# A two-layer graph network: the nodes normalised in eight groups of blocks instead of seven

## What is computed

```python
x = _layernorm(x + _L0_gnn_ref(edge_index, x))          # layer 0
x = _layernorm(x + _L1_gnn_ref(x, edge_index, edge_attr_4, edge_attr_32, ...))   # layer 1

# layer 0: out[dst] += x[src] * deg_inv_sqrt[src] * deg_inv_sqrt[dst]
# layer 1: w = relu(edge_feat @ W1 + b1) @ W2 + b2        four 8 x 8 matrices per edge
#          m = products of w, x[src] and edge_sh          32 numbers per edge
#          out[dst] += m ; out += x @ (si_w0, si_w1) / sqrt(8)

def _layernorm(x, eps=1e-05):
    m = jnp.mean(x, axis=-1, keepdims=True)
    v = jnp.var(x, axis=-1, keepdims=True)
    return (x - m) / jnp.sqrt(v + eps)
```

## Time and profile before

| | |
|---|---|
| runs | 3487.09, 3489.55, 3490.99 us (median 3489.55) |
| the profiled execution | 3488.94 us, its span 3486.2 us |
| TensorE busy | 2796.1 us, 80% of the span |
| VectorE busy | 2974.5 us, 85% |
| ScalarE busy | 1433.7 us, 41% |
| GpSimd busy | 2464.9 us, 71% |
| mean granted TensorE clock | 0.928 of full speed |
| table transfers after layer 0 | 7 of 224 KB |
| output transfers | 6 of 224 KB, one of 208 KB and one of 10.5 KB |

### The profile page before, as it was taken

How to read it: one execution, slowest core, us unless ns; L and a number is a source line. 1 busy time by engine, 2 the same in 40 slices (tenths; PEclk the granted TensorE clock), 3 DMA queues, 4 the chain that set the end, 5 groups by cost and what they waited for, 6 DMA issues and landing times.

```text
span 3486.2 us, 55367 instructions
## 1 busy us (share of the span) xinstructions
PE 2796.1 (80%) x17493; PEld 1893.0 (54%) x17493; DVE 2974.5 (85%) x6514; ACT 1433.7 (41%) x3154; POOL 2464.9 (71%) x2520
## 2 busy tenths in 40 slices
PE   5699999999999987777777787777778777877775
PEld 4477776777777764444444454444445444444443
DVE  8788888888888865988888889889889888988987
ACT  0788888888888863211121112111212121112211
POOL 0677776777777657777777777777777777777774
PEclk9999999999999997999898898999989998999988
DMA  2200000000000021111111111111111111111112
GB/s 50 29 14 14 13 14 13 14 14 13 12 14 14 13 34 22 31 27 28 27 31 27 27 27 31 27 27 28 30 27 28 27 31 27 27 28 27 31 27 34
DMA packets 181444, 85.57 MB, mean 25 GB/s; under 512 B 124024, under 2 KB 167608, under 8 KB 181176
## 3 DMA queue, kind: packets, MB, share of 16 engines
q0 software_dynamic: 79872, 41.05, 8.0%
q1 hardware_dynamic: 101304, 41.07, 5.2%
HBM read 77.13 MB, written 4.81 MB: 24 GB/s over the span
## 4 chain that ended last, share of the span: by engine, by line
POOL 39%; issue 17%; ACT 17%; PE 14%; DVE 12%; DVEq 1%; DMA 1%; POOLq 0%; SPq 0%; ACTq 0%
POOL xg L435 39%; ACT z_sb L476 9%; ACT q_sb L476 7%; PE ps L635 4%; PE ps L648 4%; PE ps L593 3%; DVE prod_all L1062 2%; DVE stage L1231 2%; PE ps L623 1%; DVE oh L949 1%; DVE prod_all L1221 1%; PE ps L739 1%; DVE sumT_all L1085 1%; DVE lane L1058 1%; DVE z_sb L841 1%
## 5 line engine op out<-in xcount | busy, mean ns | idle before, releaser
L435 POOL DMA_INDIRECT xg<-x_table,idx x1664 | 1602.5, 963 | 562.7 <-issue 531.4
L435 POOL DMA_INDIRECT xg<-scaled_x_table,idx x832 | 854.9, 1028 | 400.7 <-issue 374.5
L739 PE MATMUL ps<-w2t,hT 128*128 128x256 f32 x3328 | 899.8, 417 | 283.9 <-DVE prod_all L1221 278.9
L739 PEld LDWEIGHTS ps<-w2t,hT 128*128 128x128 f32 x3328 | 643.2, 204 | 735.7 <-issue 640.3
L635 PE MATMUL ps<-prod_all,lane 128*128 128x363 bf16 (+1 forms) x2496 | 792.5, 320 | 51.8 <-DVE prod_all L1062 35.0
L1062 DVE TENSOR_SCALAR prod_all<-wide_lane,key 128x363 bf16<-128x363 bf16 (+1 forms) x2496 | 730.4, 316 | 27.8 <-PE ps L635 23.0
L1231 DVE TENSOR_REDUCE stage<-prod_all 128x192 f32<-128x1536 f32 x416 | 724.0, 1741 | 0.2 <-issue 0.2
L523 ACT ACTIVATE hT<-ps,b 64x512 f32<-64x512 f32 x416 | 284.4, 684 | 932.7 <-PE ps L732 928.6
L476 ACT ACTIVATE q_sb<-ps 128x363 bf16<-128x363 f32 (+1 forms) x1248 | 504.7, 543 | 94.2 <-PE ps L635 87.8
L476 ACT ACTIVATE z_sb<-ps 128x363 bf16<-128x363 f32 (+1 forms) x1248 | 504.7, 543 | 85.1 <-PE ps L635 81.8
L1215 DVE TENSOR_TENSOR prod_all<-ps,stage 128x768 f32<-128x768 f32 x416 | 397.1, 955 | 143.6 <-PE ps L739 68.7
(11 more groups left out here) (128 smaller groups left out, 1528.5 us busy)
## 6 DMA issues: line engine op xcount, KB each, us to landing
efT<-in_efT SPq DMA_DIRECT2D x104, 256.0 KB
xg<-x_table,idx POOLq DMA_INDIRECT x1664
xg<-scaled_x_table,idx POOLq DMA_INDIRECT x832
sh<-in_sh SPq DMA_DIRECT2D x104, 32.0 KB
idx<-in_src SPq DMA_DIRECT2D x156, 8.0 KB
scaled_x_table<-q_sb SPq DMA_DIRECT2D x2, 784.0 KB, 7.6
x_table<-x_sb SPq DMA_DIRECT2D x7, 224.0 KB, 4.7
out_rows<-q_sb SPq DMA_DIRECT2D x6, 224.0 KB
```

Of the source, the lines that this page charges most:

```text
L435: pool.indirect_dma_start(rows[k][:, t, :], None, table, bass.IndirectOffsetOnAxis(ap=idx[k][:, t:t + 1], axis=0),).then_inc(s_g[layer][k] ...
L739: mm = pe.matmul(ps_w[j % 2][:, t, :], hT[j % 2][:, t * P:(t + 1) * P], w2t[:].rearrange("p c o i -> p (c o i)"), start=True, stop=True)
```

## The change

The group bounds are written out: `bounds = [0, 14, 28, 42, 56, 70, 84, 92, 98]`. Six groups of fourteen blocks stay; the seventh, once blocks 84 to 97, is now 84 to 91 (eight blocks), and an eighth holds the last six. All slices, the tests for the last output rows and the counts that depend on `NG` follow. `last_chunk_of(6)` is 98 and `turn_of(6)` is 50. Since the loop over the remaining groups in layer 0 now comes right behind a group that is scaled in the same buffer `z_row`, VectorE waits there for its own row.

```diff
+LAST = 6
...
-    NG = NP // GB
+    bounds = [*range(0, NP, GB), NP - LAST, NP]
+    NG = len(bounds) - 1
...
     def last_chunk_of(g):
-        return CHUNKS - 1 if g == NG - 1 else min(CHUNKS - 1, math.ceil((GB * P * (g + 1) + SLACK) / RISE) - 1)
+        return CHUNKS - 1 if g == NG - 1 else min(CHUNKS - 1, math.ceil((P * bounds[g + 1] + SLACK) / RISE) - 1)
...
         def blocks_of(t, g):
-            return t[:, g * GB:(g + 1) * GB, :]
+            return t[:, bounds[g]:bounds[g + 1], :]
...
-                for b in range(GB):
-                    col = (g * GB + b) * P
+                for b in range(bounds[g + 1] - bounds[g]):
+                    col = (bounds[g] + b) * P
                     mm = pe.matmul(ps_rows[:, b * D:(b + 1) * D], sumT[layer][:, col:col + P],
...
+            def first_rows(t, g):
+                return t[:, 0:bounds[g + 1] - bounds[g], :]
...
             def centre(layer, g, z):
-                cols = slice(g * GB, (g + 1) * GB)
+                cols = slice(bounds[g], bounds[g + 1])
                 dve.wait_ge(s_tr[layer], g + 1)
-                rows = ps_rows.rearrange("p (h f) -> p h f", f=D)
+                rows = first_rows(ps_rows.rearrange("p (h f) -> p h f", f=D), g)
...
                 for g in left:
-                    centre(0, g, z_row[:]).then_inc(s_last[0] if g == NG - 1 else s_var[0], 1)
-                    scale(0, g, z_row[:], g + 1)
+                    if g:
+                        dve.wait_ge(s_row[0], g)
+                    centre(0, g, first_rows(z_row, g)).then_inc(s_last[0] if g == NG - 1 else s_var[0], 1)
+                    scale(0, g, first_rows(z_row, g), g + 1)
```

More of the change, by code:

```diff
@@ L372, in _ @@
                 sp.wait_ge(s_row[1], g + 1)
-                a, b = g * GB, min((g + 1) * GB, full)
+                a, b = bounds[g], min(bounds[g + 1], full)
                 if b > a:
@@ L377, in _ @@
                     sent += 1
-                if a <= full < (g + 1) * GB and rest:
+                if a <= full < bounds[g + 1] and rest:
                     sp.dma_start(out_d[full * P:n_out, :], q_sb[0:rest, full, :]).then_inc(s_out, 16)
@@ L480, in deviations @@
             def deviations(layer, g):
-                cut = slice(g * GB, (g + 1) * GB)
+                cut = slice(bounds[g], bounds[g + 1])
                 act.wait_ge(s_var[layer], g + 1)
@@ L1002, in spread_over @@
             def spread_over(t, g):
-                return t[:, g * GB:(g + 1) * GB].unsqueeze(2).to_broadcast([P, GB, D])
+                return t[:, bounds[g]:bounds[g + 1]].unsqueeze(2).to_broadcast([P, bounds[g + 1] - bounds[g], D])
+            def first_rows(t, g):
+                return t[:, 0:bounds[g + 1] - bounds[g], :]
             def centre(layer, g, z):
-                cols = slice(g * GB, (g + 1) * GB)
+                cols = slice(bounds[g], bounds[g + 1])
                 dve.wait_ge(s_tr[layer], g + 1)
-                rows = ps_rows.rearrange("p (h f) -> p h f", f=D)
+                rows = first_rows(ps_rows.rearrange("p (h f) -> p h f", f=D), g)
                 if layer == 0:
@@ L1019, in centre @@
                     out=z, in0=spread_over(mean, g), scalar=-1.0 / D, in1=z, op0=ALU.mult, op1=ALU.add)))
-                dve.wait_ge(s_node[layer], link(layer, dve.tensor_tensor(z_sq[:], z, z, ALU.mult)))
-                return dve.tensor_reduce(var[:, cols], z_sq[:], AX_X, ALU.add)
+                dve.wait_ge(s_node[layer], link(layer, dve.tensor_tensor(first_rows(z_sq, g), z, z, ALU.mult)))
+                return dve.tensor_reduce(var[:, cols], first_rows(z_sq, g), AX_X, ALU.add)
             def scale(layer, g, z, made):
-                cols = slice(g * GB, (g + 1) * GB)
+                cols = slice(bounds[g], bounds[g + 1])
                 dve.wait_ge(s_std[layer], made)
@@ L1147, in _ @@
                     if centred:
-                        scale(0, centred[0], z_row[:], centred.pop() + 1)
+                        scale(0, centred[0], first_rows(z_row, centred[0]), centred.pop() + 1)
                     if left and turn_of(left[0]) == n - 1:
                         g = left.pop(0)
-                        centre(0, g, z_row[:]).then_inc(s_var[0], 1)
+                        centre(0, g, first_rows(z_row, g)).then_inc(s_var[0], 1)
                         centred.append(g)
```

## The result

The changed kernel takes 3477.86 us (median of seven runs, 3475.76 to 3480.64) beside 3489.55 us for the kernel before (3485.6 to 3492.56), a ratio of 0.9967 with a 95% interval of 0.9955 to 0.9979. The forecast was 3479.8 us. Measured twice more in later sittings it is 0.9974 (0.9964 to 0.9984) and 0.9976 (0.9967 to 0.9985), so the first ratio lies on the high side of the gain, and 8 to 9 us are the better figure. The profiled execution is the fastest of the seven: 3475.76 us, its span 3473.7 us.

A forecast was written before the change was run, and what follows sets the result against it. GpSimd's layer 1 gathers were taken as the bound: -4.6 us at layer 0's end, 0 inside layer 1, -5.0 at the program's end, -9.6 from 3488.94; with 0.6 us to the median, 3479.8 us, range 3477.0 to 3484.0.

The forecast's parts named there:

- The bound: GpSimd's uninterrupted gather stream in layer 1 leads; gains come from the end of layer 0 and the end of the program.
- Tiles' start: End of layer 0: the group of eight goes ahead of the last sixteen dense tiles, delaying their start, +2.5 us (+1.9 to +3.5).
- Less crowding: End of layer 0: later tiles meet about half the register-load crowding from table transfers, -1.1 us (0 to -2.2).
- Shorter end: End of layer 0: twelve last transposing passes -3.5 us, seven VectorE operations over 192 columns -1.9, last table transfer -0.6.
- the two prices: VectorE operation over 192 columns: 0.348 us by the profile rows, an estimated 0.36 us by the Trainium skill's fixed price.
- Inside layer 1: Chunks 100 to 103: sixteen extra passes and the group of eight's `centre` fit under VectorE's waits for rows, 0 us.
- rival 1: End of layer 1: VectorE late, 1.5 to 5 us of delay reach the end, 3481.3 to 3484.8 us; chance 0.20.
- The cover: VectorE's waits for rows of chunks 101 (0.51 us) and 102 (5.45 us), 6.0 us together, hiding the added layer 1 work.
- End of the program: After the last sums: passes -2.9 us (-1.8 at half clock), six operations -1.7, output transfer -0.4; sum -5.0 us.
- rival 2: Half clock in the last passes and no relief for the tiles: +1.1 and +1.1 us, 3482 us; chance 0.15.
- the 4.6 us less that the text named: Sign at the program's end: time from the last sums to the output transfer's issue falls by 4.6 us.
- three things that the text named as proof against it: GpSimd starting after 1310, chunk 103's features moving differently from GpSimd's start, or last twelve passes over 2 us.

The follow-up runs named there:

- idle time: Changed kernel with layer 1's transposes of all groups but the last moved behind the previous chunk's sums, where TensorE idles: 3482.05 us, 0.9986 of the kernel before.
- kept busy: Changed kernel plus 36 unread products on zeros on TensorE before layer 0's last transposes and layer 1's last sums: 3474.61 us, 0.9962 of the kernel before.
- before again: The kernel before, unedited, measured and profiled a second time: ratio 1.0001 to itself.
- layer 1 only: Kernel before with the new group bounds (eight groups) in layer 1 alone, seven groups kept in layer 0: 0.9984 of the kernel before.
- layer 0 only: Kernel before with the new group bounds (eight groups) in layer 0 alone, seven groups kept in layer 1: 0.9984 of the kernel before.
- all three edits: Changed kernel with the edits of between the tiles, idle time and kept busy together: 3474.68 us, 0.9964 of the kernel before.
- between the tiles: Changed kernel with layer 0's group of eight transposed behind the last dense products, its VectorE operations spread between the last sixteen tiles: 0.9974 of the kernel before.

## Why the prediction was right

**The bound.** Right: GpSimd's gathers waited 0.6 us for VectorE before and after, and both gains come from the two stretches outside them. A became 4.0 us shorter (mean of three profiles with the old end of layer 0, 30.38, less that of the five with the new one unaltered, 26.41); the sum had 4.6.

**Tiles' start**, +2.5 (1.9 to 3.5): the first tile came 4.70 us behind the start of the sums' addition in place of 2.56, **+2.1**. VectorE could begin at 1281.54, and the register load lay partly under `centre`: the tile had only 0.18 us of wait ahead of it.

**Less crowding**, -1.1 (0 to -2.2): the step that was off most, **-0.2** in the profile after (11.09 us for fifteen steps against 11.32). But these two profiles differ in more than the change. The table's first six transfers come behind layer 0's last gathers, and these end at one of several distances from the sums of chunk 50. The transfers, before and after:

```profile
1283.70 25.43 SPq L361 DMA_DIRECT2D x_table<-x_sb  x7
```

```profile
1283.44 19.92 SPq L363 DMA_DIRECT2D x_table<-x_sb  x8
```

They start 1.5 us behind the sums' addition before and 3.7 us behind it after, and either occurs with either kernel. Where they start 1.5 to 1.7 us behind it, fifteen steps took 11.32 us with the old order at the end of layer 0 (before) and 10.42 with the new one (idle time, kept busy), **-0.9**; the first tile came 0.3 to 0.4 us later there, so that A gained nothing more. Where they start 3.7 to 3.9 us behind it, the steps took 11.23 and 11.46 us in the old order (before again, layer 1 only) and 10.89 to 11.11 in the new one (the changed kernel three times, layer 0 only), **-0.3**. So the relief is real, and its size hangs on the place of the transfers, which the sum took as fixed. On the chip where they started over 16 us ahead of the sums' addition, the steps of the kernels with all three edits took 9.8 us, against 11.7 and 11.8 us for the same order beside the transfers (all three, between the tiles): the crowding is some 2.0 us in all, near the sum's 2.2.

**Shorter end.** Twelve passes took 2.77 us for 2.65, with the wait 3.4 us less (-3.5 in the sum). The operations over 192 columns took 0.36 us for 0.348: 3.34 us from the first to the last in place of 5.24, **-1.9** as forecast. Of the two prices, the one that the Trainium skill gives (VectorE: DVE Perf Modes, the section on the TRN2 errata), an estimated 0.36 us, is the one that the trace shows. The transfer gave **-0.4** for -0.6.

**Inside layer 1**, 0: not right. This is rival 1, and it happened in all three profiles of the changed kernel: the lag is 5.0 to 5.6 us where it was 4.5 and 3.7 before. The sixteen passes ran at half the clock (3.62 us) each time, and VectorE waited 5.5 to 5.7 us behind them. The cover shrank as well, in the way the rival named: before, the output transfers were issued at 3426.05, as the last rows of chunk 102 were to land; now they are issued 16.4 us ahead of the last gather's end in place of 21.0, and ScalarE, which takes the same rows, has them before that (gathers of chunk 102 ended at 3417.01):

```profile
3418.50 0.42 ACT L532 ACTIVATE stage<-xg 128x256 f32<-128x256 f32 x1 [3.86 <-DMA xg<-x_table,idx]
```

That is 1.5 us from the last gather's end to the rows, where it was 5.2 (3426.77 to 3431.95). In the other profiles with the old end of layer 1 the same delay was 2.2 and 4.2 us, so the cover of 5.45 us was that of one execution. The twelve profiles on the chips that ran as usual bear this out: where the first output transfer was issued within 0.8 us of the end of chunk 102's gathers, the rows came 2.1 to 5.2 us after that end, and where it was issued 3.3 us or more behind it, 1.4 to 1.5 us. The price lay at the low end of the rival's 1.5 to 5 us or below it: 0.6 us against the first profile before, 1.9 against the second, 1.2 between the means of three. Layer 1 alone shows the forecast's 0: sixteen passes at the full clock, lag 3.44.

**End of the program**, -5.0: B is 35.2 to 36.2 us in place of 37.7 to 39.1 (the three with the old end of layer 1), a mean of 2.7 us less, with the lateness in it. Without the lateness it is about 4. Of the terms, the operations gave -1.65 for -1.7 (2.95 us from the first to the last in place of 4.60), the passes -1.7 in two profiles and -2.9 in the third, where they took 1.52 us, for -2.9. So rival 2 was right in the clock in two of three. In the second profile of the changed kernel the last sums began at half the clock as well, behind the same wait of 10.12 us, but the clock came back within them, ahead of the passes (TensorE's rows, then TensorE busy, granted clock, DMA share and GB/s by stretch):

```profile
3462.28 3.61 PE L595 MATMUL ps<-oh,stage 128*64 128x76 f32 x32 [10.12 <-DVE stage L1247]
3466.66 1.52 PE L625 MATMUL ps<-places,sumT_all 64*128 64x32 f32 x12 [0.77 <-DVE sumT_all L969]
```

```profile
3463.00:3465.00 2.00, 2.00 (x19) 0.50 0.42 66
3465.00:3466.00 1.00, 0.89 (x13) 1.00 0.00 0
```

The Trainium skill's rule (TensorE: Matmul & The Clock Gate, Part 1), that the clock is throttled by default and activity releases it, agrees with this: the sums start slow behind the wait in all three profiles, and with TensorE kept at work they ran at full speed (2.32 us). It does not make the passes slow each time, as the prediction's reading of it had. The output transfer gave between 0 and -0.7 for -0.4.

From the last sums' addition to the output transfer's issue it took 6.8, 5.6 and 6.8 us in place of 10.2, so the 4.6 us less that the text named came about in one profile of three, and 3.3 us in the others.

Forecast 9.6 us, shown by the stretches 6.6, timed 11.7, 9.0 and 7.7. Two of the three things that the text named as proof against it did come about: the last twelve passes took over 2 us, and the features of chunk 103 moved by 9.0 us where GpSimd's start moved by 6.2, the rest being the shorter gathers of that execution less 0.6 us of lateness. The stretches in place of the terms would have made 3482.8, inside the range, and near the bound of 3482.6 between faster and the same; the timed runs, all three, lie below it, at 3477.0 to 3479.35. Their ratios, 0.9967, 0.9974 and 0.9976, are below the 0.998 that parts faster from the same, but the interval lies wholly below it only the first time. The 1 to 5 us between stretches and times are as large as the spread of single executions, and no run settles them. So the two places and the way the gain arises were foreseen, but that 3477.86 us lies 2 us from the forecast is in part luck: rival 1 and the clock half of rival 2 came true and took some 2 us from the end of the program, the end of layer 0 gave 0.6 us less, and 5 us that no stretch shows came on top in that timing, against 2.4 and 1.1 in the later ones.

## What to carry to other kernels

Work that can only begin when everything before it is done should be cut so that its last piece is small, but look at where the first piece goes: here a third of what the end of layer 0 gained (2.1 of some 6 us) was paid ahead of the tiles, and spreading the same operations over gaps between dependent steps gave 1.2 us of it back in the one profile taken. A cover that consists of a wait for data is not fixed, since the change itself may move what makes the data late. And where single profiles of one kernel differ by 5 us, compare stretches from a landmark inside the same execution, and leave the total to the timed runs.

## What the runs showed that was not expected

- The granted clock at the end of a layer is worth 1.2 us for twelve f32 passes (2.77 against 1.53) and 2.0 us for the 32 passes of the last sums (4.31 against 2.32), and 36 matmuls on zeros ahead of them kept it up at the end of layer 0 in four profiles of four. Ahead of the last sums they kept it up in one execution of three, and 44 of them in the one that was profiled.
- The rows of the last gather land 3.3 to 3.7 us after its end in every profile on the chips that ran as usual, where those of chunks 99 to 101 take 1.3 to 1.5 us; no edit here moved this.
- A register load of VectorE takes 0.34 us, and up to 0.75 us in the changed profile while the table's transfers run:

```profile
L1080 DVEq TENSOR_LOAD <-tile_first x16: 335/346/749, 1283.8 to 1294.9; - x16
```

- On one chip the kernel before and the two with all three edits took half as long again, with TensorE idle inside groups that wait for no other engine, and edits worth 12 us elsewhere could not be seen in the time.
